# Empty instructions on TensorE in a six-layer local-attention kernel, so that two steps are 533 and 619 instructions long

## The reference

```
for i in range(DEPTH):                        # 6 layers
    x = attn_layer(shift_tokens(x), Wqkv[i], q_scale[i], k_scale[i], Wo[i]) + x
    x = ffn_layer(shift_tokens(x), ln_g[i], ln_b[i], W1[i], b1[i], W2[i], b2[i]) + x

def attn_layer(x, Wqkv, qs, ksc, Wo):
    q, k, v = split(x @ Wqkv)                 # 16 heads of 64
    q, k = l2norm(q) * qs, l2norm(k) * ksc    # then rotated by position
    ...                                       # window 32: a query sees its window and the one before
    return softmax(8 * q k^T, masked) v @ Wo

def ffn_layer(x, g, bln, W1, b1, W2, b2):
    a, gate = split((layernorm(x) * g + bln) @ W1 + b1)
    return a * gelu(gate) @ W2 + b2
```

## Time and profile before

| | |
|---|---|
| median of 3 runs | 3296.93 us (3294.43 to 3297.98) |
| the profiled execution | 3314.26 us |
| its span, first to last instruction | 3312.4 us |
| mean granted TensorE clock | 0.977 |
| busy PE / DVE / ACT / POOL | 95% / 85% / 77% / 79% |

### The profile page before, as it was taken

How to read it: one execution, slowest core, us unless ns; L and a number is a source line. 1 busy time by engine, 2 the same in 40 slices (tenths; PEclk the granted TensorE clock), 3 DMA queues, 4 the chain that set the end, 5 groups by cost and what they waited for, 6 DMA issues and landing times.

```text
span 3312.4 us, 123078 instructions
## 1 busy us (share of the span) xinstructions
PE 3145.3 (95%) x52802; PEld 2738.7 (83%) x52802; DVE 2809.6 (85%) x3751; ACT 2550.6 (77%) x3699; POOL 2622.3 (79%) x2593
## 2 busy tenths in 40 slices
PE   7978999999999989999989999999999999999997
PEld 4647888888888878888878888888888888888886
DVE  7968888888888888888888888888888888888884
ACT  6756788777877878887878888878878777777875
POOL 6658888878878878888878888888888787878883
PEclk9989999999999999999999999999999999999997
DMA  2001111111211111121101111111111111111111
GB/s 65 2 10 37 60 38 37 34 34 41 64 37 34 41 32 42 37 63 35 41 28 47 37 58 40 34 34 43 40 58 40 33 35 39 38 34 34 41 34 37
DMA packets 57868, 129.81 MB, mean 39 GB/s; under 512 B 11120, under 2 KB 33264, under 8 KB 56560
## 3 DMA queue, kind: packets, MB, share of 16 engines
q1 hardware_dynamic: 57328, 121.94, 12.6%
HBM read 19.17 MB, written 2.10 MB: 6 GB/s over the span
## 4 chain that ended last, share of the span: by engine, by line
PE 90%; issue 4%; ACT 3%; POOL 2%; DVE 2%; DMA 0%; POOLq 0%; DVEq 0%; SPq 0%; ACTq 0%
PE pair L207 72%; PE pair L210 17%; POOL sq L395 0%; ACT qT L842 0%; ACT PT L823 0%; DVE wq_l L950 0%; DVE VB L317 0%; ACT sq L820 0%; ACT kT L859 0%; ACT oT L847 0%; POOL wq_l L950 0%; DVE qk L313 0%; ACT sq L832 0%; ACT VA L855 0%; ACT wq_h L920 0%
## 5 line engine op out<-in xcount | busy, mean ns | idle before, releaser
L1100 POOL TENSOR_TENSOR qk<-qk,ts 128x1024 f32<-128x1024 f32 x384 | 910.5, 2384 | 138.9 <-DVE ts L964 130.7
L1079 POOL TENSOR_TENSOR qk<-qk,rn 128x1024 f32<-128x1024 f32 x384 | 727.4, 1915 | 15.0
L960 DVE TENSOR_TENSOR qk<-pair,tab 128x1024 f32<-128x1024 f32 x384 | 468.5, 1220 | 271.4 <-ACT sq L820 265.8
L820 ACT ACTIVATE sq<-pair 128x1024 f32<-128x1024 f32 x192 | 197.0, 1026 | 455.4 <-PE pair L207 455.4
L207 PE MATMUL pair<-wq_h,xs_h 128*128 128x512 f32 x1154 | 516.4, 448 | 22.3 <-POOL xs_l L934 7.9
L1111 POOL TENSOR_TENSOR Sx<-Sx,rden 128x1024 f32<-128x1024 f32 x192 | 365.2, 1902 | 172.5 <-DVE rden L1026 172.5
L964 DVE TENSOR_TENSOR ts<-pair,tab 128x1024 f32<-128x1024 f32 x384 | 466.6, 1215 | 0.0
L207 PE MATMUL pair<-wq_h,xs_l 128*128 128x512 f32 x1152 | 465.1, 404 | 0.7 <-issue 0.6
L207 PE MATMUL pair<-wq_l,xs_h 128*128 128x512 f32 x1152 | 464.2, 403 | 0.3 <-issue 0.2
L968 DVE TENSOR_REDUCE ss<-sq 128x16 f32<-128x1024 f32 x384 | 464.2, 1209 | 0.0
L210 PEld LDWEIGHTS pair<-small,qk 128*128 128x128 f32 x3072 | 354.8, 144 | 84.2 <-issue 50.8
(11 more groups left out here) (127 smaller groups left out, 6711.8 us busy)
## 6 DMA issues: line engine op xcount, KB each, us to landing
VB<-VA SPq DMA_DIRECT2D x192, 384.0 KB, 3.5
VB<-VA SPq DMA_DIRECT2D x96, 128.0 KB, 3.4
wq_raw<-wqkv SPq DMA_DIRECT2D x6, 1536.0 KB, 8.5
xf<-xT SPq DMA_DIRECT2D x96, 64.0 KB, 1.9
xf<-xT SPq DMA_DIRECT2D x96, 63.8 KB, 2.0
wo_sb<-wo SPq DMA_DIRECT2D x6, 512.0 KB, 3.7
X<-x_in SPq DMA_DIRECT2D x4, 512.0 KB, 7.1
out<-X SPq DMA_DIRECT2D x16, 128.0 KB, 2.0
```

What stands on the lines that cost most here:

```text
L820: A_.activation(sq[:, 0, :], one[:, :], ACT.Square).then_inc(S["squared"], 1)
L960: V_.tensor_tensor(h3(qk[:, now, kind, :], DH), h3(source[:, :], DH), rep(tab[:, 2 * kind, b, :], HEADS, DH), ALU.mult)
L1079: G_.tensor_tensor(x, x, bc(rn[:, then, kind * HEADS:(kind + 1) * HEADS], HEADS, DH), ALU.mult).then_inc(S["scaled"], 1)
L1100: G_.tensor_tensor(qk[:, now, kind, :], qk[:, now, kind, :], ts[:, kind, :], ALU.add).then_inc(S["added"], 1)
```

## The change

Three kinds of places get calls of a new helper `idle(e, n)`, which issues n increments of the semaphore `waited`: the start of TensorE's program (239), the start of each step (`FILL`, by the step's number in its layer), and places behind matmuls and ahead of transposes, where `even` is 1 in even steps and `odd` in odd ones.

```
+        FILL = (0, 6, 1, 7, 1, 7, 1, 7, 1, 7, 1, 7, 1, 7, 1, 7, 1, 7, 1, 7, 1, 7, 1, 7, 1, 7, 1, 7, 1, 7, 1, 7)
+        FILL_AHEAD = 239
+        def idle(e, n):
+            for _ in range(n):
+                apart(e)
-        def project(pair, high, low, first):
+        def project(e, n, pair, high, low, first):
...
                 mm(out, high, wq_h[:, cols], True, False)
+                idle(e, n)
                 mm(out, low, wq_h[:, cols], False, False)
+                idle(e, n)
                 last = mm(out, high, wq_l[:, cols], False, True)
+                if u == 0:
+                    idle(e, n)
...
+            even, odd = (1, 0) if b == 0 else (0, 1)
+            idle(e, FILL[t % NBLOCKS])
...
-                project(one, high, low, 0).then_inc(S["q_done"], 1)
+                project(e, 2 * odd, one, high, low, 0).then_inc(S["q_done"], 1)
+                idle(e, 2 * odd)
...
                 for a in range(PAIRS):
+                    idle(e, odd if a else 0)
                     last = tr(PC[:, a * P:(a + 1) * P], Sx[:, then, a, :, :].rearrange("p w k -> p (w k)"))
...
-                project(other, high, low, INNER).then_inc(S["k_done"], 1)
+                project(e, 2 * odd, other, high, low, INNER).then_inc(S["k_done"], 1)
+                idle(e, 2 * odd)
...
-                project(one, high, low, 2 * INNER).then_inc(S["v_done"], 1)
+                project(e, 0, one, high, low, 2 * INNER).then_inc(S["v_done"], 1)
...
                 for a in range(PAIRS):
+                    idle(e, even if a else 0)
                     last = tr(PC[:, a * P:(a + 1) * P], qk[:, then, 1, a * P:(a + 1) * P])
...
                         mm(to, w1_h[:, at], f_h[:, :], True, False)
+                        idle(e, even)
                         mm(to, w1_l[:, at], f_h[:, :], False, False)
+                        idle(e, even)
                         last = mm(to, w1_h[:, at], f_l[:, :], False, True)
+                        if k:
+                            idle(e, even)
...
                 for a in range(PAIRS):
+                    idle(e, 2 * even if a else 0)
                     last = mm(PC[:, 0:P], wo_sb[:, a, :], oT[:, a, :], a == 0, a == PAIRS - 1)
...
         def _(pe):
+            idle(pe, FILL_AHEAD)
             pe.wait_ge(S["c_loaded"], 16)
             pe.wait_ge(S["w_centred"], 1)
             first_stage(pe, first_pe)
```

## The result

The changed kernel takes 3525.64 us (median of 4 runs, 3522.41 to 3531.32) against 3297.45 for the kernel before on the same chip: a ratio of 1.068 by the means (95% interval 1.063 to 1.073). Predicted was 3249 with a range of 3234 to 3291. The prediction was wrong, and in its sign. The stalls went away as forecast; the empty instructions cost about four times what the stalls had.

The account below looks back on a forecast made before the run. TensorE was taken to bound the kernel, stalling in AV at instruction-block borders. Stalls removed (-60), a later start (+9) and lost cover (+3) gave -48 us, from 3296.93 to 3249 us, range 3234 to 3291.

Parts of the forecast that it names:

- The bound and the stalls: TensorE bounds the kernel; its stalls in AV at 256-instruction borders cost 69 us, of which the change gains about 60.
- part (2): On TensorE one added increment was taken to cost 80 ns, between 51 ns and some 0.12 us.
- rival (b): TensorE becomes bound by its sequencer at 0.13 us an increment among matmuls: +56 us, 3353 us; chance 0.08.
- part (3): Matmuls and transposes in the steps hide the increments at 80 ns: 0 to 6 us lost, 3 taken.
- part (4): The 239 increments ahead of the first stage are not covered, so it starts 9 us late.
- The sum: Over the whole kernel, -60 + 9 + 3 = -48 us, from 3296.93 to 3249 us; chance 0.70.

Follow-up runs that it names:

- experiment 3: The changed kernel with 175 instead of 239 increments ahead of the first stage, AV at 30, 51, 158, 179 behind a border: 3603.82 us in one run.
- experiment 7: Experiment 2 with 14 odd-step increments replaced by small loads, twelve behind odd-step q and k matmuls; 51 ahead, AV at 69, 107, 197, 235: 3314.17 us, ratio 1.003.
- experiment 8: Experiment 7 with 55 instead of 51 increments ahead, AV at 73, 111, 201, 239: 3320.46 us, ratio 1.005.
- experiment 9: Experiment 2 with 62 instead of 68 increments ahead, AV at 59, 111, 187, 239: 3312.36 us, ratio 1.003.
- experiment 2: The changed kernel with its 75 increments per two steps spread singly beside matmuls, 68 ahead, AV at 65, 117, 193, 245: 3250.38 us, ratio 0.985.
- experiment 10: Experiment 8 with small loads moved from odd-step q and k to even-step v and W1, 40 more after the constants' wait: 3247.84 us, ratio 0.984.
- experiment 1: The kernel before with six runs of fillers, among them increments, met waits and small loads, at TensorE's start: 3326.59 us in one run.
- experiment 6: The changed kernel with 14 of 21 increments at the even-to-odd turn moved to v matmuls and scores, 232 ahead: 3369.92 us, ratio 1.019.
- experiment 4: The changed kernel with each increment replaced by a 32x32 weight load, places unchanged: 3286.9 us, ratio 0.996.

## Why the prediction was wrong, step by step

**The bound and the stalls: right.** Every gap that experiments 3 and 7 to 9 brought back sits at the border, wherever AV was moved; the change put AV at 94, 115, 222, 243 as counted. At the border 45 idle times (41.5 us) became ten (10.1 us). Six AVs of the last layer still stall: t = 180, 184, 187, 188, 191, 192, where 176 was named instead of 192 (behind 176 it is the v projection that comes late). The changed kernel's clean odd-to-even step at 14.79 and experiment 2 show the gain. Its size per stall, 1.6 us with the clock, is right too: between the kernels with AV at 73, experiments 8 and 10, 46 stalls make 72.6 us, 1.58 each (69.7 us and 1.51 when each is set against the kernel before on its own chip). By the Trainium skill ("Runtime: NRT & Kernel Launch", Instruction fetch mechanics) crossing a block is "mostly hidden". The trace agrees for most of the 449 packets of experiment 8, but at those 46 borders the crossing is not hidden.

**The price of one increment, part (2): the step that failed.** "So 51 ns from below, some 0.12 us from above by rounding; I take 80 ns": it was 151 ns by experiment 1. Neither row was a bound. The 51 ns are a recorded duration, which is the same for instructions that hold the sequencer 105 and 151 ns. The distance of 0.1 us came from waits on TensorE and from another engine's increments; TensorE had no two pure increments in a row in the trace. The reason for staying below a wait's price, "since nothing is polled", points the wrong way: a pure increment is the dearer of the two. All that was set against rival (b), at 0.08, was POOL's pair.

**The cover, part (3): the limits hold, the price of losing them does not.** The limits were 117 ns for q and k, 113 for PT, 118 for W1, 109 for the turn, and 151 is above all of them. Put into the same sums it gives 21 x 0.151 - 2.3 = 0.9 at the turn (measured 0.98), 6 x (0.302 - 0.234) = 0.41 in each of q and k (0.52 and 0.46), 7 x (0.151 - 0.113) = 0.27 in PT (0.28): 2.0 of the 2.4 us by which a clean even-to-odd step grew (15.37 to 17.76 in the median). W1 and the transposes of k make up 0.2 more. The prediction had priced the case without cover at up to 0.15 us for each of q, PT and k, 30 to 40 us in all. By these sums every increment beyond the cover pays in full, and it was 2.4 us a pair, some 230 us in 96. The lead that experiment 6 points to was missing too: it makes a stretch free until it is used up, and a turn that uses it up makes all that follows pay. Without it the expectation of experiment 6 was 60 to 70 us short.

**The start, part (4): right in kind.** Nothing covers it, as said; 27 us late instead of 9.

**The sum.** With the measured start and the measured 2.4 us a pair it would have been -60 + 27 + 96 x 2.4 = +197 us, and with the 2.0 that follow from the price alone +159; the trace has +217, and what is left is not assigned. Rival (b) is what happened. It was priced at 0.13 us and came out at 3353, 170 us too fast; its point of decision, about 115 ns, agrees with 151, but no run has a price near it. The tests named in the prediction worked: the first load at 37.63 is past "25 us or later", and a pair of clean steps takes 32.5, past 30.6.

## What to carry to other kernels

Price an instruction by the distance between the starts of two of its kind on its own engine, never by its recorded duration; where the trace has no such pair, rows of another kind are no bound, and the case where it is twice as dear needs its full chance. Padding for position is cheap only where each filler stands beside work that is longer than it: here 75 increments cost nothing when they stood one by one beside matmuls, and 2.4 us per two steps when crowded. Where a place modulo a block decides, keep well away from the edges of the bad zone, since what stands ahead moves them.

## What the runs showed of the hardware

A pure increment holds TensorE's sequencer 151 ns and a met wait on two semaphores about 105, both recorded as 51 (experiment 1). A run of 256 small instructions in 2 us stalls for about a microsecond in its middle when it begins close behind a border of 256 instructions, and not when it begins further on (experiments 3 and 7 to 10). 32x32 weight loads follow each other at 27 ns and are all but hidden among large matmuls (experiment 4), yet with twelve of them in the odd step's q and k 46 of 47 AVs at 73 stall, and with these moved away none of 47.
